# Projecting K ahead of Q, evacuating on VectorE, and projecting most of Q and all of V inside the first part of attention, in a causal transformer layer

## The chip, the cores and the metric

The kernel is one program that runs on the 8 cores of one Trainium2 chip. Each core computes two of the 16 sequences, one after the other, with no exchange between cores. The metric is device time in microseconds (us) of the slowest core, as a median of runs.

## The reference

One layer: causal attention with 16 heads, a layer norm over input plus attention, then a quantised linear layer and a second layer norm.

```python
def _L0_attn_ref(x, WQ, WK, WV, WO):            # x: (16, 2048, 1024), 16 heads of 64
    Q = _split_heads(x @ WQ.T, h)
    K = _split_heads(x @ WK.T, h)
    V = _split_heads(x @ WV.T, h)
    scores = jnp.einsum('bhqd,bhkd->bhqk', Q, K) / jnp.sqrt(jnp.float32(dk))
    scores = jnp.where(causal, scores, NEG)
    m = jnp.max(scores, axis=-1, keepdims=True)
    e = jnp.exp(scores - m)
    attn = e / jnp.sum(e, axis=-1, keepdims=True)
    out = jnp.einsum('bhqk,bhkd->bhqd', attn, V)
    return out @ WO.T
def _L0_ffn_ref(x, w_int8, weight_scale, bias):
    w_deq = w_int8.astype(jnp.float32) * weight_scale
    x_norm = simple_rms_norm(x)
    x_q = activation_quant(x_norm)
    return jnp.einsum('bsd,od->bso', x_q, w_deq) + bias
x = _layernorm(x + _L0_attn_ref(x, ...), axis=-1)
x = _layernorm(x + _L0_ffn_ref(x, ...), axis=-1)
```

## The kernel before

Every sequence ("batch" below) has S = 2048 rows and D = 1024 columns. The instruction stream of each engine is written out by hand: `emit(engine, fn)` appends work, `W(engine, key, val)` appends one wait of that engine on a semaphore (each call is an instruction of its own, also where the value has been reached long before), and `bump` counts what has been signalled. So an engine's order is the order of the calls. PE is TensorE, DVE VectorE, ACT ScalarE, POOL GpSimd.

A batch runs through three functions. `ph1` loads the transposed input `xT` (four DMAs) and the weights for Q and K into the two weight buffers `wslot[0]` (wslotA in the trace) and `wslot[1]` (wslotB), and projects. A projection group is 8 matmuls that accumulate a 128x512 tile in one PSUM bank. Q has 64/2 = 32 groups and K has 32; they rotate over PSUM banks 0 to 3, and ACT copies each tile to `QT` or `KT` (line 283). Then `ph1` defines `emit_vgroup`, a group of the V projection: 8 matmuls (line 318) into bank 6 or 7 and a DVE copy into `Vx` (line 331). There are 32 of these. WV is loaded to `wslot[0]` once Q's last matmul is done.

`ph2` is attention. It loops over four query chunks `qc` of 512 rows, over eight head pairs `hp`, and over `n_kt = 4*qc + 4` key tiles `k`: 4, 8, 12 or 16 steps in a head pair, 320 in a batch, 32 of them in qc = 0. Step `u` does this:

- PE: `emit_st` waits until ACT has read the same half of the double buffer two steps earlier (one wait), then issues two score matmuls (64 rows, up to 512 columns, line 381) into PSUM banks 2p and 2p+1, p = u % 2. In the last four steps of a head pair the columns shrink: 512, 384, 256, 128.
- ACT: exp of the scores into `PT` (line 482 at full width, line 493 narrower).
- POOL: in the last four steps of a head pair, the causal mask on two 128x128 blocks (line 507).
- PE: two steps later, `emit_pv` (line 399) multiplies with `Vx` into banks 4 and 5, after a wait on the mask of an earlier step.

At the end of a head pair PE waits for the last exps and masks, issues the remaining small products, and DVE normalises them into `o_ring` (lines 544 to 557). In qc = 0 three V groups follow each head pair (eight V groups stand ahead of the first); in qc >= 1 a transpose of an earlier chunk's output follows (`emit_trans`, line 425). The second linear layer's weights are loaded to `wslot[1]` as `ph2` begins, WO to `wslot[0]` after the first head pair of qc = 1; both DMAs are issued by POOL. `ph45` is the output projection, the norms and the quantised layer; the change does not touch it.

Of the kernel before, what the change touches and what calls it, by code (L numbers as in the profile page):

```python
# [38 lines left out]
def build_nc():  # L39
# [13 lines left out]
    with ExitStack() as ctx:  # L53
# [164 lines left out]
        def ph1(b, v_ready, prev_t_end, prev_v_end, prev_s_end):  # L218
# [10 lines left out]
            xt_done = ctr["gx"]  # L229
# [12 lines left out]

            wq_done = wload(wq_h, 0, prev_t_end)
            wk_done = wload(wk_h, 1, prev_t_end)

            s_evac = {}
            v_evac = {}
            half = 0
            q_last_mm = 0
# [3 lines left out]
            for proj, (wdone, slot, dest) in enumerate(  # L253
                    ((wq_done, 0, QT), (wk_done, 1, KT))):
                W("t", wdone[0], wdone[1])
                if proj == 0:
                    W("t", "gx", xt_done)
                    W("t", "v", v_ready)
                    W("t", "v", prev_v_end)
                    W("t", "s", prev_s_end)  # L260
                for dt in range(8):
                    for sch in range(4):
                        if half >= 4:
                            W("t", "s", s_evac.get(half - 4))
                        def f(eng, dt=dt, sch=sch, half=half, slot=slot):
                            out = pslot(half)
                            for kt in range(8):
                                lhsT = wslot[slot][
                                    :, kt * 1024 + dt * 128:
                                    kt * 1024 + dt * 128 + 128]  # L270
                                rhs = xT[:, kt * 2048 + sch * 512:
                                         kt * 2048 + (sch + 1) * 512]
                                mm = eng.matmul(out, lhsT, rhs,  # L273
                                                start=(kt == 0),
                                                stop=(kt == 7),
                                                skip_group_check=True)
                                if kt == 7:
                                    mm.then_inc(sem_t, 1)
                        emit("t", f)
                        mmv = bump("t")  # L280
                        W("s", "t", mmv)
                        def f3(eng, dt=dt, sch=sch, half=half, dest=dest):
                            eng.copy(dest[:, dt * 2048 + sch * 512:  # L283
                                          dt * 2048 + (sch + 1) * 512],
                                     pslot(half)).then_inc(sem_s, 1)
                        emit("s", f3)
                        s_evac[half] = bump("s")
                        half += 1
                if proj == 0:
                    q_last_mm = ctr["t"]  # L290

            wv_done = wload(wv_h, 0, q_last_mm)
# [10 lines left out]
            def emit_vgroup(g):  # L303
                st, dc = g // 2, g % 2
                n = ppu["n"]
                ppu["n"] += 1
                phh = n % 2
                if g < 2:
                    W("t", wv_done[0], wv_done[1])
                W("t", "v", ppu["ev"].get(n - 2))  # L310
                def f(eng, st=st, dc=dc, phh=phh):
                    out = pp[:, phh * 512:(phh + 1) * 512]
                    for kt in range(8):
                        lhsT = xT[:, kt * 2048 + st * 128:
                                  kt * 2048 + st * 128 + 128]
                        rhs = wslot[0][:, kt * 1024 + dc * 512:
                                       kt * 1024 + (dc + 1) * 512]
                        mm = eng.matmul(out, lhsT, rhs, start=(kt == 0),  # L318
                                        stop=(kt == 7),
                                        skip_group_check=True)  # L320
                        if kt == 7:
                            mm.then_inc(sem_t, 1)
                emit("t", f)
                mmv = bump("t")
                W("v", "t", mmv)
                def f2(eng, st=st, dc=dc, phh=phh):
                    dst = ap(Vx, st * 1056 + dc * 8 * 66,
                             (16896, 128), (66, 8), (1, 64))
                    src = ap(psall, 3072 + phh * 512, (4096, 128),
                             (64, 8), (1, 64))  # L330
                    eng.tensor_copy(dst, src).then_inc(sem_v, 1)  # L331
                emit("v", f2)
                val = bump("v")
                ppu["ev"][n] = val
                v_upto[st] = val

            qk_last_s = s_evac[63]
            return qk_last_s, vones, emit_vgroup, v_upto

        def ph2(b, wait_s0, vones, emit_vg, v_upto):  # L340
# [11 lines left out]
            w8_done = wload2(w8_h, 1, ctr["t"])  # L352
# [9 lines left out]
            for g in range(8):  # L362
                emit_vg(g)
            vg_next = 8
            prev_evac = max(vones, v_upto[3])

            def emit_st(qc, hp, k, p, wait_s):
                W("t", "s", wait_s)
# [73 lines left out]
            for qc in range(4):  # L442
                for hp in range(8):
                    if hp == 0:
                        W("t", "v", v_upto[min(4 * qc + 3, 15)])
# [6 lines left out]
                    for k in range(n_kt):  # L452
                        p = u % 2
                        pt = u % 4
                        wait_s = expv.get(u - 2)
                        if wait_s is None and u < 2:
                            wait_s = wait_s0
                        if u < 2:
                            W("t", "v", vones)
                        emit_st(qc, hp, k, p, wait_s)  # L460
                        stv = ctr["t"]
                        if k >= 2:
# [9 lines left out]
                            if mms:  # L472
                                W("t", "g", maskv.get(uu - 1))
                                if ku == 0:
                                    W("t", "v", prev_evac)
# [22 lines left out]
                        exp_last[p] = expv[u]  # L498
                        if k >= 4 * qc:
# [15 lines left out]
                    for ku in (n_kt - 2, n_kt - 1):  # L515
# [10 lines left out]
                        if mms:  # L526
                            emit_pv(qc, hp, mms, n_started, n_total)
# [39 lines left out]
                    if qc == 0:  # L567
                        while vg_next < min(32, 8 + 3 * (hp + 1)):
                            emit_vg(vg_next)
                            vg_next += 1  # L570
                    if qc >= 1:
# [3 lines left out]
                        if wo_done is None:  # L575
                            wo_done = wload2(wo_h, 0, ctr["t"])
# [360 lines left out]
        prev_s_end = 0  # L937
        for b in range(BPC):
            qk_s, vones, emit_vg, v_upto = ph1(b, v_ready, prev_t_end,
                                               prev_v_end, prev_s_end)  # L940
            (trans_done, wo_done, w8_done, exp_last,
             trans_ev) = ph2(b, qk_s, vones, emit_vg, v_upto)
# [4 lines left out]
            prev_s_end = ctr["s"]  # L947

# [65 lines left out]
```

## Time and profile before

| | us |
|---|---|
| median of two runs | 1715.0 (1714.69 to 1715.3) |
| the profiled execution | 1715.27 |
| its span on the slowest core, core 5 | 1713.4 |
| spans of the eight cores | 1697.5 to 1713.4 |
| mean granted TensorE clock by core | 0.799 to 0.817 of 2.4 GHz |

The profile is of core 5. In batch 0 the DMA of the first inputs lasts until 48 us, the Q and K projections until 161, eight V groups until 175, qc = 0 until 277, qc = 1 until 356, qc = 2 until 480, qc = 3 until 617 and `ph45` until 855; batch 1 repeats this. "The granted clock" is the share of full clock that TensorE was given: it is either 1.2 or 2.4 GHz, so 0.77 is a mix of both.

### The profile page before, as it was taken

How to read it: one execution, taken by the hardware profiler on the slowest of the kernel's cores; microseconds unless marked ns; L12 is line 12 of the kernel's file. 1: busy time of each engine (PE TensorE's matmuls, PEld its weight loads, DVE VectorE, ACT ScalarE, POOL GpSimd, SP SyncE). 2: the span in 40 equal slices, each digit the busy share in tenths (PEclk: the TensorE clock that was granted, in tenths of full speed). 3: DMA queues.
4: the chain of work that ended last, by engine and by line, in shares of the span. 5: the costliest groups of instructions: out<-in, count | busy, mean ns of one | idle time of the engine just before them, and what ended most of it. 6: DMA issues, size and time to landing. Idle time of an engine off the chain costs nothing.

```text
span 1713.4 us, 25217 instructions; the slowest of 8 cores (1697.5 to 1713.4 us)
## 1 busy us (share of the span) xinstructions
PE 1237.7 (72%) x8710; PEld 584.4 (34%) x8710; DVE 576.1 (34%) x1647; ACT 854.1 (50%) x1188; POOL 302.6 (18%) x599
## 2 busy tenths in 40 slices
PE   1899777877777776667409997877777777756664
PEld 0344333434344332222204443333443434322221
DVE  1000322211111148888600012322111111588886
ACT  0332224777788743444503322156777878334444
POOL 1000222222211211221200002232222121111112
PEclk9999876577778888888759997765677887888887
DMA  9331102000000002222192220020000000022211
GB/s 159 62 50 22 28 1 47 4 1 2 1 2 1 1 13 62 77 87 83 67 164 40 50 50 1 1 50 1 2 1 1 1 2 1 25 68 80 74 62 62
DMA packets 21917, 64.54 MB, mean 38 GB/s; under 512 B 1315, under 2 KB 1315, under 8 KB 21796
## 3 DMA queue, kind: packets, MB, share of 16 engines
q0 software_dynamic: 17184, 46.14, 12.9%
q1 hardware_dynamic: 4612, 16.78, 3.4%
q8 instruction: 76, 1.25, 0.3%
q14 instruction: 45, 0.37, 0.1%
HBM read 75.50 MB, written 16.78 MB: 54 GB/s over the span
## 4 chain that ended last, share of the span: by engine, by line
PE 40%; ACT 20%; DVE 14%; POOL 10%; issue 9%; DMA 5%; DVEq 1%; ACTq 0%; POOLq 0%
ACT PT L482 19%; PE psall L273 13%; POOL PT L507 9%; PE psall L318 8%; PE psall L641 8%; DMA wslotA<-wqt 5%; PE psall L381 5%; PE psall L399 4%; DVE dump L679 2%; DVE dumpb L682 2%; PE psall L425 2%; DVE st L685 1%; DVE st L686 1%; DVE z2x L842 1%; DVE z L842 1%
## 5 line engine op out<-in xcount | busy, mean ns | idle before, releaser
L482 ACT ACTIVATE PT<-psall,ebias 128x1024 bf16<-128x1024 f32 x448 | 468.5, 1116 | 308.8 <-PE psall L381 308.8
L381 PE MATMUL psall<-QT,KT 64*128 64x512 bf16 (+3 forms) x1280 | 280.9, 450 | 126.8 <-ACT PT L482 112.1
L399 PE MATMUL psall<-Vx,PT 128*128 128x65 bf16 x4352 | 303.0, 216 | 85.4 <-POOL PT L507 83.9
L507 POOL TENSOR_TENSOR PT<-PT,mask 128x128 bf16<-128x128 bf16 x512 | 200.6, 425 | 703.6 <-ACT PT L482 703.3
L399 PEld LDWEIGHTS psall<-Vx,PT 128*128 128x128 bf16 x4352 | 210.0, 110 | 246.9 <-issue 235.9
L544 DVE RECIPROCAL rinv<-psall 128x4 f32<-128x4 f32 x64 | 11.7, 183 | 636.5 <-PE psall L399 636.5
L641 PE MATMUL psall<-wslotA,OT 128*128 128x512 bf16 x512 | 159.1, 483 | 80.5 <-DVE z L842 44.5
L273 PE MATMUL psall<-xT,wslotA 128*128 128x512 bf16 x512 | 114.6, 388 | 86.3 <-DMA wslotA<-wqt 86.3
L331 DVE CAST Vx<-psall 128x512 bf16<-128x512 f32 x64 | 44.3, 692 | 382.6 <-PE psall L318 381.2
L825 PE MATMUL psall<-wslotB,qT 128*128 128x512 bf16 x512 | 123.8, 398 | 42.3 <-ACT qT L809 42.3
L318 PE MATMUL psall<-wslotA,xT 128*128 128x512 bf16 x512 | 147.0, 457 | 0.0
L381 PEld LDWEIGHTS psall<-QT,KT 64*128 64x128 bf16 x1280 | 68.2, 97 | 228.5 <-issue 206.6
L493 ACT ACTIVATE PT<-psall,ebias 128x768 bf16<-128x768 f32 (+2 forms) x192 | 120.8, 697 | 0.0
L641 PEld LDWEIGHTS psall<-wslotA,OT 128*128 128x128 bf16 x512 | 59.3, 119 | 179.4 <-issue 151.2
L273 PE MATMUL psall<-xT,wslotB 128*128 128x512 bf16 x512 | 110.8, 379 | 0.0
L557 DVE TENSOR_SCALAR o_ring<-psall,rinv 128x64 bf16<-128x64 f32 x512 | 104.3, 277 | 5.8 <-issue 0.8
L273 PEld LDWEIGHTS psall<-xT,wslotA 128*128 128x128 bf16 x512 | 50.8, 100 | 151.2 <-issue 93.5
L283 ACT CAST QT<-psall 128x512 bf16<-128x512 f32 x64 | 37.5, 586 | 117.7 <-PE psall L273 117.7
L825 PEld LDWEIGHTS psall<-wslotB,qT 128*128 128x128 bf16 x512 | 49.7, 101 | 106.5 <-issue 58.4
L726 ACT ACTIVATE sc<-sc 128x2 f32<-128x2 f32 x32 | 6.5, 204 | 158.9 <-DVE sc L717 158.9
L318 PEld LDWEIGHTS psall<-wslotA,xT 128*128 128x128 bf16 x512 | 56.8, 113 | 82.6 <-issue 44.7
L783 POOL TENSOR_TENSOR x1b<-x,bias_b 128x1024 f32<-128x1024 bf16 x32 | 68.4, 2137 | 73.5 <-DVE qint L773 68.1
(95 smaller groups left out, 886.1 us busy)
## 6 DMA issues: line engine op xcount, KB each, us to landing
xstg<-x SPq DMA_DIRECT2D x32, 512.0 KB, 3.7
y<-outst POOLq DMA_DIRECT2D x32, 512.0 KB, 3.0
xT<-xt POOLq DMA_DIRECT2D x8, 1024.0 KB, 21.4
wslotA<-wqt POOLq DMA_DIRECT2D x2, 2048.0 KB, 41.5
wslotB<-wkt POOLq DMA_DIRECT2D x2, 2048.0 KB, 52.2
wslotA<-wvt POOLq DMA_DIRECT2D x2, 2048.0 KB, 16.5
wslotB<-w8t POOLq DMA_DIRECT2D x2, 2048.0 KB, 16.1
wslotA<-wot POOLq DMA_DIRECT2D x2, 2048.0 KB, 15.0
```

What stands on the lines that cost most here:

```text
L273: mm = eng.matmul(out, lhsT, rhs, start=(kt == 0), stop=(kt == 7), skip_group_check=True)
L318: mm = eng.matmul(out, lhsT, rhs, start=(kt == 0), stop=(kt == 7), skip_group_check=True)
L331: eng.tensor_copy(dst, src).then_inc(sem_v, 1)
L381: last = eng.matmul(out, lhsT, rhs, start=True, stop=True, skip_group_check=True)
L399: last = eng.matmul(out, lhsT, rhs, start=(i_glob < 2), stop=(i_glob >= n_total - 2), skip_group_check=True)
L482: eng.activation(PT[:, pt * 1024:(pt + 1) * 1024], psall[:, p * 1024:(p + 1) * 1024], AF.Exp, bias=ebias[:, :], scale=0.125).then_inc(sem_ ...
L493: eng.activation(dst, src, AF.Exp, bias=ebias[:, :], scale=0.125).then_inc(sem_s, 1)
L507: last = eng.tensor_tensor(blk, blk, mask01[:, :], ALU.mult)
L557: last = eng.tensor_scalar(o_ring[:, ro + qt * 1024 + h * 64: ro + qt * 1024 + h * 64 + 64], ps[:, qt * 65:qt * 65 + 64], rinv[:, s_ * 4 + ...
L641: mm = eng.matmul(out, lhsT, rhs, start=(dt == 0), stop=(dt == 7), skip_group_check=True)
L783: eng.tensor_tensor(x1b2h(t), x1[:, t * 1024:(t + 1) * 1024], bias_b2[:, 0:1024], ALU.add).then_inc(sem_m, 1)
L825: mm = eng.matmul(out, lhsT, rhs, start=(dt == 0), stop=(dt == 7), skip_group_check=True)
```

## The change

- K is projected ahead of Q. Its weights are loaded first, and its groups run with the column chunk `sch` outside and `dt` inside. Q's first column chunk (8 groups) follows. The other 24 Q groups are emitted inside attention, two after each of the steps u = 0 to 11.
- `proj_group` evacuates with DVE in place of ACT. It waits on whatever last read its PSUM bank, which is kept in `slotc`. A Q group emitted in step u uses bank 2p or 2p+1, which hold the scores of step u, so it waits for the exp of step u.
- All 32 V groups are emitted inside attention, two after each of the steps u = 0 to 15. None stands ahead of attention, and none follows a head pair.
- `emit_st` waits four times where it waited once: on `slotc` of its two banks (in most steps the same value of the same semaphore), on the evacuation of its K chunk and on that of its Q chunk. In qc = 0 the products wait for their V tile as well.
- WV goes to `wslot[1]` after K's last matmul, WO to `wslot[0]` after Q's last group in qc = 0, and the second layer's weights to `wslot[1]` after the first head pair of qc = 1. POOL still issues all three.
- The memset of the ones column of `Vx` stands behind 40 evacuations on DVE; it gates the first two score steps.

```diff
+            evK = {}
+            evQ = {}
+            H = {"half": 0, "first_ev": True, "q_all": None}
+            slotc = [None, None, None, None]
...
+            def proj_group(slot, dt, sch, dest, ev):
+                j = H["half"] % 4
+                if slotc[j] is not None:
+                    W("t", slotc[j][0], slotc[j][1])
+                def f(eng, dt=dt, sch=sch, j=j, slot=slot):
+                    out = pslot(j)
+                    for kt in range(8):
...
+                emit("t", f)
+                mmv = bump("t")
+                W("v", "t", mmv)
+                if H["first_ev"]:
+                    H["first_ev"] = False
+                    W("v", "t", prev_t_end)
+                    W("v", "g", prev_m_end)
+                def f3(eng, dt=dt, sch=sch, j=j, dest=dest):
+                    eng.tensor_copy(dest[:, dt * 2048 + sch * 512:
+                                         dt * 2048 + (sch + 1) * 512],
+                                    pslot(j)).then_inc(sem_v, 1)
+                emit("v", f3)
+                ev[(dt, sch)] = bump("v")
+                slotc[j] = ("v", ev[(dt, sch)])
+                H["half"] += 1
+
+            W("t", wk_done[0], wk_done[1])
+            W("t", "gx", xt_done)
+            W("t", "v", v_ready)
+            W("t", "v", prev_v_end)
+            W("t", "s", prev_s_end)
+            for sch in range(4):
                 for dt in range(8):
...
+                    proj_group(1, dt, sch, KT, evK)
+            k_last_mm = ctr["t"]
+            wv_done = wload(wv_h, 1, k_last_mm)
+
+            W("t", wq_done[0], wq_done[1])
+            for dt in range(8):
+                proj_group(0, dt, 0, QT, evQ)
+            qrem = [(dt, sch) for sch in (1, 2, 3) for dt in range(8)]
+            qst = {"i": 0}
+
+            def emit_qgroup():
+                dt, sch = qrem[qst["i"]]
+                qst["i"] += 1
+                proj_group(0, dt, sch, QT, evQ)
+                if qst["i"] == len(qrem):
+                    H["q_all"] = ctr["t"]
...
-                        rhs = wslot[0][:, kt * 1024 + dc * 512:
+                        rhs = wslot[1][:, kt * 1024 + dc * 512:
...
-            w8_done = wload2(w8_h, 1, ctr["t"])
+            w8_done = None
...
-            for g in range(8):
-                emit_vg(g)
-            vg_next = 8
-            prev_evac = max(vones, v_upto[3])
-
-            def emit_st(qc, hp, k, p, wait_s):
-                W("t", "s", wait_s)
+            vg_next = 0
+            prev_evac = vones
+
+            def emit_st(qc, hp, k, p):
+                for j in (2 * p, 2 * p + 1):
+                    if slotc[j] is not None:
+                        W("t", slotc[j][0], slotc[j][1])
+                W("t", "v", evK[(hp, k // 4)])
+                W("t", "v", evQ[(hp, qc)])
...
-                        wait_s = expv.get(u - 2)
-                        if wait_s is None and u < 2:
-                            wait_s = wait_s0
                         if u < 2:
                             W("t", "v", vones)
-                        emit_st(qc, hp, k, p, wait_s)
+                        emit_st(qc, hp, k, p)
...
+                                if qc == 0:
+                                    W("t", "v", v_upto.get(ku))
...
+                        slotc[2 * p] = ("s", expv[u])
+                        slotc[2 * p + 1] = ("s", expv[u])
+                        if qc == 0:
+                            nst = u + 1
+                            while qst["i"] < min(nq, 2 * nst):
+                                emit_qgroup()
+                            if qst["i"] == nq and wo_done is None:
+                                wo_done = wload2(wo_h, 0, P["H"]["q_all"])
+                            while vg_next < min(32, 2 * nst):
+                                emit_vg(vg_next)
+                                vg_next += 1
...
-                    if qc == 0:
-                        while vg_next < min(32, 8 + 3 * (hp + 1)):
-                            emit_vg(vg_next)
-                            vg_next += 1
                     if qc >= 1:
...
-                        if wo_done is None:
-                            wo_done = wload2(wo_h, 0, ctr["t"])
+                        if w8_done is None:
+                            w8_done = wload2(w8_h, 1, ctr["t"])
```

## Rows read from the trace of the kernel before

**Rows 1.** Busy time by stage of batch 0; first line: the columns.
```profile
core 5: us, PE busy (x) PEld busy (x) DVE busy (x) ACT busy (x) POOL busy (x), PEclk, DMA share, GB/s
48.00:175.00 127.00, 126.51 (x576) 56.75 (x576) 4.92 (x8) 38.79 (x65) 1.75 (x2) 1.00 0.28 43
175.00:277.00 102.00, 78.92 (x420) 33.08 (x420) 31.63 (x105) 22.83 (x32) 25.06 (x64) 0.77 0.04 7
277.00:356.00 79.00, 60.55 (x568) 31.16 (x564) 17.95 (x78) 56.71 (x64) 25.18 (x63) 0.59 0.16 28
356.00:480.00 124.00, 94.40 (x978) 49.55 (x978) 22.27 (x99) 97.80 (x104) 25.91 (x67) 0.72 0.01 1
480.00:617.00 137.00, 101.84 (x1146) 54.49 (x1142) 17.76 (x80) 113.31 (x121) 25.11 (x64) 0.81 0.01 1
```

**Rows 2.** Chain that ended last: start us, us, what. Projections and V bursts, batch 0.
```profile
48.31 112.69 PE psall L273 x512
161.01 13.83 PE psall L318 x64
...
181.27 7.41 PE psall L318 x24
...
268.90 7.93 PE psall L318 x24
```

**Rows 3.** The same chain: start of attention, then the second head pair of qc = 0.
```profile
174.93 0.70 DVE Vx L331
175.63 0.35 issue
175.97 0.41 PE psall L381 x2
...
189.11 1.12 ACT PT L482
...
193.64 0.27 PE psall L399 x2
```

**Rows 4.** PE in order of time, the same head pair: its first scores.
```profile
188.62 0.55 PE L381 MATMUL psall<-QT,KT 64*128 64x512 bf16 x4
```

**Rows 5.** Instructions of qc = 0 by shape: count, busy us, mean ns, idle before.
```profile
L331 DVE CAST Vx<-psall 128x512 bf16<-128x512 f32 x25 | 17.3, 692 | 32.9 <-PE psall L318 32.9
...
L482 ACT ACTIVATE PT<-psall,ebias 128x1024 bf16<-128x1024 f32 x8 | 8.9, 1114 | 82.4 <-PE psall L381 82.4
L493 ACT ACTIVATE PT<-psall,ebias 128x768 bf16<-128x768 f32 x8 | 7.1, 893 | 0.0
...
L493 ACT ACTIVATE PT<-psall,ebias 128x512 bf16<-128x512 f32 x8 | 5.5, 688 | 0.0
L493 ACT ACTIVATE PT<-psall,ebias 128x256 bf16<-128x256 f32 x8 | 3.8, 474 | 0.0
```

**Rows 6.** Other engines in order of time: ACT's table load; DVE's memset of `Vx`.
```profile
51.97 1.28 ACT L283 ACT_TABLE_LOAD   x1 [51.97 <-PE psall L273]
...
14.80 0.27 DVE L296 MEMSET Vx<- 128x256 bf16 x1 [0.86 <-issue]
```

**Rows 7.** DMA issues at 100 to 182 us: KB, us to landing.
```profile
wslotA<-wvt POOLq DMA_DIRECT2D x1, 2048.0 KB, 18.1
```

**Rows 8.** Chain inside a head pair of qc = 3: one wait of PE on an exp.
```profile
535.05 1.11 ACT PT L482
536.16 0.14 issue
```

**Rows 9.** PE in order of time, qc = 3: two steps, clock low; two steps, high.
```profile
529.03 0.60 PE L381 MATMUL psall<-QT,KT 64*128 64x512 bf16 x2
...
530.12 0.60 PE L381 MATMUL psall<-QT,KT 64*128 64x512 bf16 x2
...
535.29 0.39 PE L381 MATMUL psall<-QT,KT 64*128 64x512 bf16 x2 [0.27 <-ACT PT L482]
...
536.30 0.39 PE L381 MATMUL psall<-QT,KT 64*128 64x512 bf16 x2 [0.26 <-ACT PT L482]
```

## Prediction: time of the changed kernel, and why

> **What bounds the kernel now.** I read the stages by time first, then the chain that ended last, then PE in order of time. The reader is to see in the first that no engine is busy throughout attention (PE in 102 of 137 us of qc = 3, ACT in 113 [rows 1]), so that each stage must be read by what its chain waits for. Three kinds of stage are touched.
>
> The projections are PE and nothing else. PE is busy for 126.5 of 127 us at full clock, and 512 matmuls take 112.69 us; the 64 matmuls of eight V groups take 13.83 us, 0.216 us each [rows 1, 2]. ACT's copies are hidden under this.
>
> The stage qc = 0 alternates. After each burst of 24 V matmuls comes a stretch in which PE waits for exp and mask. It lasts from 188.68, where the burst of 7.41 us ends, to 193.91, where the next starts: 5.23 us [rows 2, 3]. Eight such stretches cost 42 us. They also cost clock: the stage has 0.77 of it, and the eight bursts take 7.4, 7.9, 6.5, 7.4, 7.9, 6.5, 7.4 and 7.9 us, 58.9 in all (first and last in [rows 2]), where 192 x 0.216 = 41.5 would do. So 17.4 us a batch is the low clock after the idle stretches.
>
> In qc = 1 to 3, ACT and PE hand each other the two score buffers. At full clock a step takes 1.00 us and PE idles 0.26 of it for the exp, so ACT bounds it; at the low clock a step takes 1.09 us and PE has no gap [rows 9].
>
> **The change, part by part.** All sums are for one batch and then doubled. They start from the profiled execution, 1715.27 us, which stands 0.3 us above the median.
>
> *Projections.* K and Q's first chunk are 40 groups, 320 matmuls. Taking 192 x 0.216 = 41.5 from the 112.69 leaves 71.2 us. A DVE evacuation takes 0.69 us and a group 8 x 0.216 = 1.73, so DVE keeps up and four banks hide it [rows 2, 5]. The start waits for the same inputs and one weight matrix as before. WV lands 18.1 us after its issue [rows 7]; between K's last matmul and the first V group stand 13.8 us of Q, the first scores and exp, and two Q groups, 20 us, so it is just covered. If it slipped, each us would show once. The later weight loads have stages to spare, and POOL issues one of them where it issued one before.
>
> *Start of attention.* Before, last matmul to first score took 1.1 us: the copy of 0.70, then 0.35 for three waits [rows 3]. Now the memset of 0.27 [rows 6] and more waits follow the copy: 1.6 us. ACT's table load of 1.28 us, hidden under the projections in batch 0 [rows 6], now stands ahead of the first exp: once 1.3 us.
>
> *qc = 0, head pairs 0 to 2.* Each of the 12 steps has scores, exp, then 32 matmuls. The Q group waits for the exp, since it takes the bank. From first score to exp is 0.49 us in full width [rows 3, 4], and I take 0.41 on average for narrower ones; the exps are 1.11 + 0.89 + 0.69 + 0.47 [rows 5]; back to PE is 0.14 [rows 8]. Four steps: 4 x 0.41 + 3.16 + 4 x 0.14 = 5.4 us. The bursts hide the masks. With 0.2 for the last products a head pair costs 5.6 + 128 x 0.216 = 33.2, three cost 99.6.
>
> *Head pair 3.* V only, banks of its own, so the exp is hidden: 64 x 0.216 + 1.2 for scores and products = 15.0.
>
> *Head pairs 4 to 7.* Nothing fills them. They cost the old 5.23 plus three more waits of PE ahead of their first score and a low clock's slower score: 5.7 each, 22.8.
>
> Sum from 48.3 us to qc = 1: 71.2 + 1.6 + 99.6 + 15.0 + 22.8 = 210.2. Before it was 228.5 (48.3 to 276.8, the end of the last burst [rows 2]). **Gain 18.3 a batch, 36.6 less 1.3 for the table, so 35.3.** Nearly all of it is clock, on the reading that PE's short stretches of 0.9 to 1.7 us between bursts are not what the 5.2 us ones are, and that the Q and V bursts run at 0.216. If instead the clock fell as it does now, the gain would be gone (a rival).
>
> *The four waits of `emit_st`.* One satisfied wait costs PE's queue something: three in a row stand for 0.35 us in the chain, one for 0.14, so each further one costs 0.105 [rows 3, 8]. Three more are 0.32 us ahead of each score pair. Where PE's queue is ahead of its array (during transposes and bursts) they cost nothing; behind an exp that has just ended they are on the way. The buffer loop spans two steps: exp 1.11 + 0.14 + scores 0.39 + about 0.10 to the exp = 1.74 against 2.00 at full clock, so 0.32 more makes 2.06, or 1.03 a step, +0.03. At the low clock it is 1.11 + 0.14 + 0.60 + 0.10 = 1.95 against 2.18, so 2.27, 1.14 a step, +0.05 [rows 8, 9]. At each head pair's start there is no such slack: about 0.1 to 0.16 for the first score, and 0.3 to 0.4 for the third, which waits on the first exp. At its end POOL's eight masks run back to back and shift no further. With 4, 8 and 12 steps between, a head pair loses 0.75, 0.9 and 0.95 us in qc = 1, 2, 3. **Eight of each: 20.8 a batch, 41.6.** Bounds: nothing, if the queue hides all the waits; 288 steps x 0.16 = 46 a batch, 92, if the loop had no slack anywhere.
>
> By the Trainium skill (Advanced Engine Details and Errata, section Network/Comms) a sequencer's read of a semaphore takes 50 to 100 ns. Three such reads would be 0.15 to 0.3 us, and as an estimate from that page the time would be 1710 to 1729; the 0.105 of the trace lies just above the page's figure.
>
> *Clock in qc = 2 and 3.* It is 0.59, 0.72 and 0.81 in the three stages [rows 1]. Longer steps hold more idle time of PE, and qc = 1, which has the shortest head pairs and so the largest part of waiting, has the lowest clock; so part of the high stretches may go. A high step that turns low costs 1.14 - 1.03 = 0.11. All of them, about half of 224 a batch, would be 25 to 27 us in both batches; I take 10. Bounds: 0 and 27.
>
> **Sum:** 1715.3 - 35.3 + 41.6 + 10 = 1731.6, and I say 1731, 0.9% slower than the median. The output projection and the norms stay.
>
> **Rivals.**
> 1. *The extra waits are free* (faster). They would have to be passed while PE's array works. For it: PE runs ahead in bursts. Against: in [rows 9] PE idles on the exp at full clock, and the queue can't pass a wait behind the one that blocks it. Time: 1715 - 35 = 1680, with some loss left 1680 to 1695. It decides at a cost per wait under about 0.03 us: then the loss is below 12 us. Chance 0.14.
> 2. *The clock falls in the new bursts* (slower). For it: after 5.2 us stretches it falls eight times a batch, and each burst loses 17.4/8 = 2.2 us. Against: the new stretches are a third as long. If all 24 bursts lost 2.2, the time is 1731 + 52 = 1783; with a third of them, 1749. The point is where a 1.7 us stretch already brings 1.2 GHz. Chance 0.08. The Trainium skill has a rule on this side (TensorE: Matmul & The Clock Gate, section A second HAM failure mode: psum-queue depth-cycling): a matmul kernel that cycles PSUM banks, with short idles between groups, can swing between the two clocks. That is the shape of the new bursts; the projections in [rows 1] cycle four banks at 1.00 of the clock, but without idles.
> 3. *The clock stays low through qc = 2 and 3*: the 27 in place of 10, with a somewhat larger wait loss, 1748 to 1755. For it: qc = 1 sits near 0.5 already. Chance 0.15.
> 4. My forecast, 1708 to 1748: 0.63.
>
> **How the numbers follow.** About 2% (34 us) is what a measurement of this kernel tells from no change; the edges are 1681 and 1749. Faster: half of rival 1 lies below 1681 or near it, and I give 0.06. Slower: rival 2's upper part, half of rival 3, and a tail of the forecast, together 0.18. Within 2%: 0.76. The range of 1696 to 1757 leaves out most of rivals 1 and 2, 0.2 in all; the forecast's own range is 1708 to 1748.
>
> **What the changed profile would show.** (a) The chain from 48 us to qc = 1 is 210 us in place of 228, and Q and V bursts run at 0.216 a matmul with a clock near 1.0 until head pair 4. (b) From exp to score the "issue" piece is 0.46 in place of 0.14. (c) Steps in qc = 3 last 1.03 and 1.14. (d) The clock in qc = 2 and 3 is below 0.72 and 0.81. (e) One table load of 1.3 us ahead of batch 0's first exp. If (b) shows less than 0.2, or if a burst of 32 matmuls takes over 8 us, the forecast is wrong.

## The result, and the profile after

| | before | after |
|---|---|---|
| median, us | 1715.3 | 1739.5 |
| ratio, 95% interval | | 1.0142 (1.0128 to 1.0156) |
| profiled execution, span of the slowest core | 1713.4 (core 5) | 1737.4 (core 6) |

The changed kernel is 1.4% slower. The forecast was 1731, 0.9% slower. The stages, in us, as means over the eight cores for batch 0 / batch 1 (from the first matmul of the projections to the first exp, then from first exp to first exp of each chunk; the last chunk to its last exp; "rest" up to the next batch or the end):

| | projections | qc = 0 | qc = 1 | qc = 2 | qc = 3 | rest |
|---|---|---|---|---|---|---|
| before | 128.2 / 129.5 | 96.6 / 96.0 | 81.1 / 80.7 | 113.1 / 113.2 | 142.7 / 143.1 | 286.0 / 248.5 |
| after | 75.4 / 75.6 | 144.1 / 144.1 | 85.5 / 85.3 | 120.6 / 120.3 | 151.6 / 151.5 | 285.6 / 246.1 |

Projections and qc = 0 together became 5.3 and 5.8 us shorter, the other three chunks 20.8 and 20.1 us longer. For the slowest cores alone it is 8.5 and 9.2 us shorter against 21.1 and 20.8 us longer.

The stages of the changed kernel, batch 0, core 6 (columns as in [rows 1]):

```profile
48.00:120.00 72.00, 71.28 (x320) 31.66 (x318) 27.60 (x40) 0.00 (x0) 0.88 (x1) 1.00 0.31 47
120.00:268.00 148.00, 122.98 (x676) 55.46 (x676) 52.60 (x133) 26.26 (x33) 26.64 (x65) 0.91 0.11 18
268.00:353.00 85.00, 63.92 (x576) 33.75 (x574) 18.98 (x87) 59.20 (x64) 26.27 (x65) 0.56 0.16 26
353.00:474.00 121.00, 94.74 (x898) 49.70 (x896) 19.73 (x89) 93.90 (x96) 25.34 (x64) 0.63 0.01 1
474.00:626.00 152.00, 115.88 (x1203) 61.71 (x1202) 19.44 (x86) 127.12 (x128) 23.69 (x60) 0.72 0.01 2
```

On these two cores the clock of qc = 0 rose from 0.77 to 0.91, and that of qc = 2 and 3 fell from 0.72 and 0.81 to 0.63 and 0.72. As means over the eight cores, between the exps that bound the stages, it is 0.82, 0.56, 0.74 and 0.79 in qc = 0 to 3 before, and 0.91, 0.54, 0.65 and 0.72 after.

PE in order of time inside a head pair of qc = 3, changed kernel (it answers to the last two of [rows 9]):

```profile
541.28 0.39 PE L412 MATMUL psall<-QT,KT 64*128 64x512 bf16 x2 [0.19 <-issue]
...
542.38 0.39 PE L412 MATMUL psall<-QT,KT 64*128 64x512 bf16 x2 [0.36 <-issue]
...
543.39 0.39 PE L412 MATMUL psall<-QT,KT 64*128 64x512 bf16 x2 [0.26 <-issue]
...
544.45 0.39 PE L412 MATMUL psall<-QT,KT 64*128 64x512 bf16 x2 [0.32 <-issue]
```

The steps are 1.10, 1.01 and 1.06 us. What is to be seen is the bracket: before, PE's idle time ended with ACT's exp; now it ends with "issue". The exp that the step waits for has ended 0.46 us before its first score (median in qc = 3, all cores), where the kernel before has 0.144 at full clock. In that time PE works through waits that are already satisfied.

The chain that ended last, changed kernel: start of attention, two of the first bursts, then the third score pair of qc = 1.

```profile
47.57 71.73 PE psall L266 x320
...
119.39 0.69 DVE QT L280
120.08 0.86 issue
...
121.79 0.41 PE psall L412 x2
122.27 1.28 ACT L512
123.56 1.12 ACT PT L512
124.82 5.04 PE psall L266 x16
129.85 3.45 PE psall L336 x16
...
134.72 3.61 PE psall L266 x16
138.34 3.45 PE psall L336 x16
...
158.07 0.70 DVE Vx L349
...
269.18 0.49 issue
269.67 0.61 PE psall L412 x2
```

What held back the first score is DVE's memset behind the copy, with idle time of its own in the bracket:

```profile
120.95 0.27 DVE L314 MEMSET Vx<- 128x256 bf16 x1 [0.86 <-issue]
121.79 0.39 PE L412 MATMUL psall<-QT,KT 64*128 64x512 bf16 x2 [2.50 <-DVE Vx L314]
```

The last two lines of the chain are the wait cost in one place: 0.49 us from exp to score where one wait stands for 0.14 [rows 8].

### The profile page after: what moved, and what is told of

Same layout as the page of the kernel before. It is cut to its first block, busy times and chain, and to the rows that moved or that the text cites. A ratio compares the mean times of both kernels' runs of the same rounds, so it can differ in the third digit from the quotient of the medians.

```text
span 1737.4 us, 27201 instructions; the slowest of 8 cores (1729.0 to 1737.4 us)
## 1 busy us (share of the span) xinstructions
PE 1257.0 (72%) x8710; PEld 601.2 (35%) x8710; DVE 663.8 (38%) x1775; ACT 808.6 (47%) x1060; POOL 305.5 (18%) x599
## 4 chain that ended last, share of the span: by engine, by line
PE 39%; DVE 19%; ACT 18%; POOL 9%; issue 7%; DMA 5%; DVEq 1%; ACTq 0%; POOLq 0%
ACT PT L512 16%; PE psall L266 14%; POOL PT L548 9%; PE psall L680 8%; PE psall L336 6%; PE psall L412 6%; DMA wslotB<-wkt 5%; PE psall L430 4%; DVE o_ring L600 4%; DVE dump L718 2%; DVE dumpb L721 2%; DVE OT L467 2%; DVE st L724 1%; DVE st L725 1%; DVE z L881 1%
## 5 line engine op out<-in xcount | busy, mean ns | idle before, releaser
L512 ACT ACTIVATE PT<-psall,ebias 128x1024 bf16<-128x1024 f32 x448 | 485.1, 1113 | 225.7 <-PE psall L412 218.1
L412 PE MATMUL psall<-QT,KT 64*128 64x512 bf16 (+3 forms) x1280 | 304.4, 478 | 135.4 <-DVE OT L467 48.5
L430 PE MATMUL psall<-Vx,PT 128*128 128x65 bf16 x4352 | 314.5, 223 | 59.1 <-POOL PT L548 55.1
L430 PEld LDWEIGHTS psall<-Vx,PT 128*128 128x128 bf16 x4352 | 222.6, 114 | 232.6 <-issue 218.6
L680 PE MATMUL psall<-wslotA,OT 128*128 128x512 bf16 x512 | 160.2, 486 | 79.3 <-DVE z L881 44.0
L523 ACT ACTIVATE PT<-psall,ebias 128x768 bf16<-128x768 f32 (+2 forms) x192 | 131.3, 686 | 168.8 <-PE psall L412 164.5
L266 PE MATMUL psall<-xT,wslotB 128*128 128x512 bf16 x512 | 115.2, 389 | 85.5 <-DMA wslotB<-wkt 85.5
L412 PEld LDWEIGHTS psall<-QT,KT 64*128 64x128 bf16 x1280 | 78.3, 98 | 246.2 <-issue 230.0
L266 PE MATMUL psall<-xT,wslotA 128*128 128x512 bf16 x512 | 120.6, 392 | 24.0 <-ACT PT L523 13.3
L680 PEld LDWEIGHTS psall<-wslotA,OT 128*128 128x128 bf16 x512 | 59.6, 120 | 179.1 <-issue 151.6
L336 PE MATMUL psall<-wslotB,xT 128*128 128x512 bf16 x512 | 115.8, 379 | 0.0
L266 PEld LDWEIGHTS psall<-xT,wslotB 128*128 128x128 bf16 x512 | 51.0, 100 | 150.7 <-issue 93.3
L280 DVE CAST KT<-psall 128x512 bf16<-128x512 f32 x64 | 44.3, 692 | 153.0 <-PE psall L266 153.0
L280 DVE CAST QT<-psall 128x512 bf16<-128x512 f32 x64 | 44.3, 692 | 106.9 <-PE psall L266 106.9
## 6 DMA issues: line engine op xcount, KB each, us to landing
xT<-xt POOLq DMA_DIRECT2D x8, 1024.0 KB, 21.1
```

What stands on the lines that cost most here:

```text
L266: mm = eng.matmul(out, lhsT, rhs, start=(kt == 0), stop=(kt == 7), skip_group_check=True)
L280: eng.tensor_copy(dest[:, dt * 2048 + sch * 512: dt * 2048 + (sch + 1) * 512], pslot(j)).then_inc(sem_v, 1)
L336: mm = eng.matmul(out, lhsT, rhs, start=(kt == 0), stop=(kt == 7), skip_group_check=True)
L412: last = eng.matmul(out, lhsT, rhs, start=True, stop=True, skip_group_check=True)
L430: last = eng.matmul(out, lhsT, rhs, start=(i_glob < 2), stop=(i_glob >= n_total - 2), skip_group_check=True)
L512: eng.activation(PT[:, pt * 1024:(pt + 1) * 1024], psall[:, p * 1024:(p + 1) * 1024], AF.Exp, bias=ebias[:, :], scale=0.125).then_inc(sem_ ...
```

## The experiments

**One wait a step again.** Which part of the change lengthens qc = 1 to 3?

```diff
-                        W("t", slotc[j][0], slotc[j][1])
-                W("t", "v", evK[(hp, k // 4)])
-                W("t", "v", evQ[(hp, qc)])
+                        W("t", slotc[j][0], slotc[j][1], once=True)
+                W("t", "v", evK[(hp, k // 4)], once=True)
+                W("t", "v", evQ[(hp, qc)], once=True)
```

`once=True` leaves a wait out if that engine has already waited for as high a value of the semaphore.

> The changed kernel, in which emit_st leaves out each wait whose value PE has already waited for on that semaphore; nothing else differs. My theory (three satisfied waits a step, 0.105 us each, lengthen the buffer loop of qc = 1 to 3): each score pair of qc 1 to 3 is again behind one wait, the stages fall back to 81, 113 and 143 us, about 20.5 us a batch, and the time is about 1699, 0.99 of the kernel before. Rival (the longer stages come from the clock, which fell in qc = 2 and 3 for another reason, or from the weight load that moved into qc = 1): the waits hardly matter and the time stays at 1735 to 1740.

Measured: 1693.9 us, ratio to before 0.9875 (0.9835 to 0.9914). The stages qc = 1, 2, 3 are 81.1, 113.1, 142.7 and 81.2, 113.4, 142.9 us, the old ones to 0.5 us. So leaving the waits out takes back 40.4 of the 40.9 us that the two batches had lost there. The clock of qc = 2 and 3 is back as well (0.74 and 0.79, means over the cores), so it fell by no cause of its own, and the moved weight load costs nothing that shows. The kernel as a whole is 45.6 us faster than the changed one, 5 more than I had forecast: qc = 0 takes 141.7 and 141.9 us where it took 144.1, so the waits cost some 4.6 us there too.

**The same waits in the kernel before.**

```diff
                 W("t", "s", wait_s)
+                if qc >= 1:
+                    for _ in range(3):
+                        W("t", "s", wait_s)
```

> The kernel before, with the one wait of emit_st written four times in qc = 1 to 3 and nothing else. My theory: its stages qc = 1, 2, 3 become those of the changed kernel, 85, 120.5 and 151.5 us, and the time 1715 + 41 = 1756. Rival (waits are nearly free and something else in the change made the stages longer): under 1725.

Measured: ratio 1.0217 (1.0163 to 1.0271, from two runs), profiled execution 1752.4 us. Stages 84.9, 120.6, 151.1 and 85.6, 120.3, 151.0, within 0.6 us of the changed kernel's. Its clock in qc = 2 falls too: 0.60 to 0.68 on the eight cores in both batches, where the kernel before has 0.74 on every core. Nothing but the waits differs, so the fall of the clock follows from them.

**Six more, and one more.** The same edit with `range(6)`, and with one line.

> The kernel before, with the one wait of emit_st written seven times in qc = 1 to 3. My theory (a loop of two steps with slack): with three more waits part of the cost lay in the slack (0.26 us at full clock), with six more it lies outside, so the cost per wait rises: full-clock steps go to 1.19 us and low-clock ones to 1.30, stages qc = 1, 2, 3 to about 95, 135 and 172 us, 65 a batch, and the time to about 1845. Rival (each wait costs the same everywhere): twice the cost of three, 1797.

> The kernel before, with the one wait of emit_st written twice in qc = 1 to 3. With three more waits the steps of qc = 3 took 1.052 and 1.140 us, so the buffer loop of two steps has 2.104 - 0.318 = 1.79 us of its own at full clock and 1.96 at the low one, against 2.00 and 2.19 measured without them. My theory (slack of 0.2 us): one more wait leaves the steps at 0.997 and 1.093 and costs only at the start of each head pair, 0.1 to 0.2 us: 5 to 9 us in all, about 1722. Rival (each wait costs the same wherever it stands): a third of the 41 us, 1729.

Measured: six give 1862.3 us (a single run, without an interval), stages 95.6, 138.5, 176.8; one gives ratio 1.003 (1.0019 to 1.0042), stages 81.8, 114.0, 144.0. The table has, over all cores, the time from the end of a head pair's first exp to its third score (median, qc = 1 to 3), where PE has nothing left to do but wait; the mean step from one exp's start to the next in seven steps in the middle of qc = 3's head pairs, at either clock; and the added time of the three stages, as the mean of the batches:

| extra waits | exp to third score, us | step at 2.4 GHz, us | step at 1.2 GHz, us | added in qc = 1 to 3, us a batch |
|---|---|---|---|---|
| 0 | 0.144 | 1.000 | 1.093 | |
| 1 | 0.250 | 1.006 | 1.094 | 2.8 |
| 3 (changed kernel) | 0.462 | 1.047 | 1.159 | 20.4 |
| 6 | 0.795 | none left | 1.301 | 73.8 |

(The last column is the sum of the stages less 336.95, the mean of before.) The steps are means because with extra waits long and short ones alternate (1.50 and 1.13 us with six), so that a median depends on the steps chosen; the 1.052 and 1.140 in the expectation are such medians. The wait itself has a fixed price, 0.106 us for each of the first three (0.250 - 0.144, and (0.462 - 0.144)/3). What it costs the stage is another matter: one wait costs 2.8, three cost 6.8 each, six cost 12.3 each. It is a loop with slack. At 1.2 GHz the slack is to be seen directly: in the middle of qc = 3 the score pair starts 0.361 us after its exp without extra waits, 0.364 with one, and 0.462 with three, so the first is hidden behind PE's own work and the others are not. With six, no step in the middle ran at full clock any more: the mean clock is 0.70 to 0.71 against 0.80 to 0.82. That is more than I had forecast, 1845, since I had counted some full-clock steps.

**V ahead of Q within a step.**

```diff
                             nst = u + 1
-                            while qst["i"] < min(nq, 2 * nst):
-                                emit_qgroup()
-                            if qst["i"] == nq and wo_done is None:
-                                wo_done = wload2(wo_h, 0, P["H"]["q_all"])
                             while vg_next < min(32, 2 * nst):
                                 emit_vg(vg_next)
                                 vg_next += 1
+                            while qst["i"] < min(nq, 2 * nst):
+                                emit_qgroup()
+                            if qst["i"] == nq and wo_done is None:
+                                wo_done = wload2(wo_h, 0, P["H"]["q_all"])
```

> The changed kernel with one thing swapped: in steps 0 to 15 of qc = 0 the two V groups are emitted ahead of the two Q groups. V's banks are free, so its 3.45 us run while ACT does the exp that the Q groups wait for. My theory (each of the 12 steps with Q groups has PE idle for the exp, 1.75, 1.42, 1.15 and 0.89 us in a head pair, 5.2 in all): 3 x 5.2 = 15.6 us a batch less, qc = 0 from 144 to 128 us, time about 1708. Rival (these idle stretches are not what keeps qc = 0 long, but the clock or the evacuations on DVE): under 5 us a batch, 1730 or more.

Measured: 1716.8 us, ratio to before 1.0007 (0.999 to 1.0023); qc = 0 takes 132.4 and 130.8 us, 11.7 and 13.3 less. So PE's idle time over the exp accounts for most of the 15.6 us a batch that I had forecast. The chain of this kernel, core 0, names two things that I had not counted:

```profile
105.83 17.14 DMA wslotB<-wvt
123.10 5.30 PE psall L336 x16
...
209.73 3.47 PE psall L266 x16
213.24 0.47 issue
213.73 0.94 POOL wslotA L378
214.68 0.83 POOL PT L548 x2
216.24 0.61 PE psall L412 x2
216.85 4.95 PE psall L336 x16
```

V now starts early enough to wait for WV's DMA. And POOL's issue of WO's load (0.94 us) waits for Q's last group and holds back the mask of that step. PE idles near 3 us there, and the next burst starts at the low clock (4.95 where 3.45 is normal). In the changed kernel the V burst stands behind Q's last group and covers this.

**V spread over qc = 0.** The first experiment and the last one together, with `min(32, 2 * nst if nst <= 4 else nst + 4)` for V.

> The changed kernel with the redundant waits of emit_st left out, V groups ahead of Q groups, and V spread: two groups in each of the first four steps, then one in each of steps 4 to 27. So head pairs 4 to 6 have a V group over each exp too. My theory: 41 us less for the waits, and qc = 0 loses nearly all idle time, from 144 to about 113 us a batch, together about 1638. Rival (the projections inside attention are bound by something other than PE's idle time over exps and masks, such as the clock or DVE's copies): the two parts don't add up, and it is 1665 or more.

Measured: ratio 0.9633 (0.9582 to 0.9685), profiled span 1649.6 us. qc = 0 takes 120.9 and 118.9 us, not 113. The direction held, and the size was over-estimated as in the step before. POOL's issue of WO's load stands in the same step as there; what part of the missing 6 to 8 us a batch it is, no run shows.

**V spread, in the kernel before, alone.**

```diff
                         exp_last[p] = expv[u]
+                        if qc == 0 and vg_next < 32:
+                            emit_vg(vg_next)
+                            vg_next += 1
...
-                    if qc == 0:
-                        while vg_next < min(32, 8 + 3 * (hp + 1)):
-                            emit_vg(vg_next)
-                            vg_next += 1
```

> The kernel before with one thing moved: the 24 V groups that follow the head pairs of qc = 0 in threes stand one after each of its first 24 steps. Q, K, ACT's copies and the single wait of emit_st stay. My theory (idle time of PE over exps and masks, and the low clock after it, is what makes qc = 0 long, and V groups over the exps are enough to remove it): 41.4 us of matmuls, some 12 of scores and products, two bare head pairs of 5.5, so 65 where 96 us were, time about 1655. Rival (the changed kernel's gain needs Q inside attention, or ACT freed of its copies): under 10 us a batch, 1695 or more.

Measured: 1647.2 us, ratio 0.9596 (0.9577 to 0.9616). qc = 0 falls from 96.6 and 96.0 to 64.5 and 63.2 us. Time beyond 0.216 us a matmul in its V bursts is 0.1 to 0.8 us a batch; in the kernel before it is 7.0 to 17.3, depending on the core. The clock of the stage is 0.96 on the slowest core:

```profile
175.00:240.00 65.00, 59.68 (x417) 26.52 (x415) 29.40 (x96) 24.93 (x32) 24.80 (x62) 0.96 0.07 13
```

So neither Q inside attention nor DVE's copies are needed for the gain.

**No wait of PE twice, in the kernel before.** The rule of the first experiment, for all of PE's waits.

> The kernel before, in which every wait of PE for a value that it has already waited for on the same semaphore is left out (the mask wait in the steps that have no mask, above all). My theory (a satisfied wait costs only where PE's queue has no slack): these stand behind the scores, where PE's queue has time to spare, so the gain is 0 to 8 us, 1707 to 1715. Rival (each satisfied wait costs 0.105 us wherever it stands, some 200 of them a batch): 20 us a batch, about 1675.

Measured: 1707.4 us, ratio 0.9947 (0.993 to 0.9964), at the upper end of the gain that I gave and far from the rival's 1675. Nearly all of it is in qc = 1 to 3, 3.9 us a batch. The place decides what a wait costs.

**ACT's copies back.** K and Q's first chunk are copied by ACT, the other 24 Q groups by DVE.

```diff
-                    proj_group(1, dt, sch, KT, evK)
+                    proj_group(1, dt, sch, KT, evK, "s")
...
-                proj_group(0, dt, 0, QT, evQ)
+                proj_group(0, dt, 0, QT, evQ, "s")
```

> The changed kernel, with K and Q's first column chunk copied out of PSUM by ACT as before, the 24 Q groups inside attention still by DVE. My theory (of the move to DVE only the start of attention is on the path): batch 0 no longer has ACT's table load of 1.28 us ahead of its first exp, and the memset no longer stands behind the last copy; 1.5 to 2 us less in batch 0 and up to 0.5 in batch 1, about 1737.5. Rival (the move to DVE holds PE up within the projections): the projections get shorter by more than 2 us a batch, 1734 or less.

Measured: 1728.9 us, ratio to before 1.0077 (1.0064 to 1.0089), some 10 us faster than the changed kernel (9.3 in the mean span of the cores). I was wrong by far. The rival's time came true and its cause did not: from the first to the last projection matmul it is 71.3 and 71.0 us here, 71.1 and 71.3 in the changed kernel. What went is the pause behind them. From the start of the last projection matmul to the first score it is 0.31 us where the changed kernel has 2.9; the table load went in batch 0; and qc = 0 itself is 2.4 and 1.1 us shorter. The chain of this kernel, core 3:

```profile
120.30 0.29 ACT QT L277
120.58 0.20 issue
120.78 1.13 ACT PT L523
121.91 0.14 issue
122.04 3.61 PE psall L266 x16
```

The Q half of the first burst takes 3.61 us, on all eight cores in batch 0, and not the 5.04 to 6.57 of the changed kernel. In batch 1, where the table load stays and the pause is 3.25 us, it takes 5.30 on seven cores. So the pause at the start of attention had cost clock as well.

**Q in the idle ends of head pairs.** PE waits for nothing twice. Q's groups use banks 6 and 7 as V's do. The second chunk stands in steps 28 to 31 and at four ends of qc = 0, the third and fourth at the ends of qc = 1 and 2. WO's load moves with the last Q group, to the head pairs of qc = 2. The second version is its base, with Q and WO's load as in the changed kernel. Of the edits of the first, the one at the ends:

```diff
...
+                    if (qc == 0 and hp < 4) or qc in (1, 2):
+                        emit_qgroup()
                     for ku in (n_kt - 2, n_kt - 1):
```

> Built on the version with V spread over qc = 0 and V ahead: PE waits for no value twice, and Q's groups use PSUM banks 6 and 7 like V's, so none waits for an exp. Q's second column chunk stands in qc = 0 (four in steps 28 to 31, four at the ends of head pairs), its third and fourth at the ends of the head pairs of qc = 1 and 2, ahead of the products that wait for POOL's masks. My theory: 16 groups a batch go into idle time of about 2 us at each end, 16 x 1.73 = 28 us less a batch of which the low clock gives some back, and qc = 0 loses its waits for the exp: 1590 to 1605. Rival (the ends of head pairs are bound by PE at the low clock, so the groups add their own time there): about the 1650 of the spread version.

> The version with V spread over qc = 0, where in addition PE waits for no value twice on any semaphore; it differs from the version with Q at the ends of head pairs (1570.6) only in where the Q groups stand and which PSUM banks they use. My theory (most of the step from 1651 to 1570.6 comes from Q's place and banks): the left-out waits bring what they brought in the kernel before, some 9 us, so about 1642. Rival (the waits left out everywhere are what made that version fast): under 1615.

Measured: 1570.6 us, ratio 0.9151 (0.9135 to 0.9168), and 1642.9 for the base, ratio 0.9568 (0.9554 to 0.9583). So Q's place and banks, with WO's load behind them, brought 72 us, more than I had forecast; the runs don't part the three. qc = 0 takes 86.3 and 84.0 us where the base has 120.7 and 119.6. qc = 1 and 2 carry eight more groups each and take 81.9, 109.1 and 80.2, 109.5, against 79.3, 111.2 and 79.5, 112.0 of the base. The stages of qc = 1 and 2, batch 0, core 5, first of the base:

```profile
245.00:324.00 79.00, 59.72 (x575) 30.75 (x572) 19.20 (x87) 56.63 (x65) 25.95 (x66) 0.63 0.16 28
324.00:435.00 111.00, 84.38 (x897) 44.67 (x896) 19.80 (x88) 89.49 (x97) 24.69 (x65) 0.74 0.01 1
```

And with Q's groups in them:

```profile
210.00:292.00 82.00, 64.60 (x647) 33.70 (x646) 24.76 (x96) 55.99 (x65) 26.13 (x66) 0.87 0.16 27
292.00:401.00 109.00, 87.77 (x955) 47.38 (x954) 24.58 (x96) 87.58 (x95) 23.67 (x61) 0.88 0.01 1
```

The clock is 0.87 and 0.88, where it is 0.63 and 0.74 in the base. So 16 groups, 28 us of matmuls a batch at 0.216 each, cost next to nothing in these stages: PE's idle time over the masks became work, and the clock rose. The runs don't part these two. In qc = 3, which holds no Q groups, the clock is 0.80 against 0.78, and its time is the same to 0.5 us.

## Why the prediction was right, and where it was not

*The sign and the time.* 1731 against 1739.5. The mechanisms were right in the main, but the time came out close in part by luck: the gain up to qc = 1 was put 17.6 us too large, and waits and clock together 9.7 us too large (51.6 against 41.9 on the slowest cores), so that the two errors partly cancelled: 1731.6 + 17.6 - 9.7 is 1739.5.

*The four waits of `emit_st`: 41.6 us, and 10 for the clock.* The first experiment gives 40.4 for both together. The mechanism was right: a further wait is 0.106 us, the loop has slack, and the knee is where it was put. The steps lengthened a little more than forecast, to 1.047 and 1.159 us where 1.03 and 1.14 stood. A head pair lost 0.56, 0.91 and 1.08 us in qc = 1, 2 and 3, with the clock's part in it, where the forecast had 0.75, 0.9 and 0.95 without it. So the shortest head pairs, which are nearly all start and end, were over-estimated. An estimate of the clock's part: leave out the first two and the last two steps of each head pair of qc = 1 to 3. Of the others that ran wholly at one clock, 52% were at full clock before and 40% after. There are 192 of them a batch and a low one is 0.11 us longer, so 0.12 x 192 x 0.11 = 2.5 us a batch, and about 5 of the 41 are clock, not 10. The two parts can't be told apart more closely, as no run has the three waits without the fall of the clock.

The figure of the Trainium skill (Advanced Engine Details and Errata, section Network/Comms: 50 to 100 ns to read a semaphore) lies a little under the 0.106 that the traces show for each further wait.

*The gain up to qc = 1: 35.3 us.* This is the term that was mis-sized most: 17.7 us on the slowest cores, 11.1 in the mean. By its own steps, for batch 0 of core 6 (forecast, then measured): projections 71.2, 71.7; start 1.6, 2.5; head pairs 0 to 2 with the table load 100.9, 106.7; head pair 3 15.0, 15.8; head pairs 4 to 7 22.8, 23.0. The sum is 211.5 against 219.8.

- The start: 0.86 us of "issue" stood between DVE's copy and the memset. It is in the bracket of the very row that I quoted for the memset [rows 6], and I read only its duration. With the rest of the pause it cost clock too: the Q half of the first burst took 5.04 us and not 3.61. The run with ACT's copies shows that this part of the change cost some 10 us in all, where I had 2.3: 1.3 for the table load and 0.5 a batch for memset and waits.
- Head pairs 0 to 2: the low clock in the first burst of head pair 0, and in that of head pair 1 (5.30), 3.1 us; the last products of head pair 0 wait for a V tile that has only just been projected, 0.70 for the copy and about 1.3 in all, which I did not count. The 16 matmuls with which a burst begins take 3.61 us and not 16 x 0.216 = 3.46, near 1.9 in the 12 bursts. Together these are 6.3 us where the head pairs came out 5.8 over the forecast, so the rest of them was a little shorter.
- The waits: the first experiment takes 2.4 and 2.2 us a batch off qc = 0 by leaving them out. I had counted them at the start and in head pairs 4 to 7 alone.
- The low clock before: I took 17.4 us from core 5. It was 17.3 and 16.3 there, but it lies anywhere between 7.0 and 17.3 over the cores and batches, for the same work. In the changed kernel it is 2.5 to 4.9, Q's bursts included. The mean gain is therefore smaller than that of the slowest core.

*The rivals.* The waits were not free. The clock did not fall in the new bursts as a rule: it was 0.95, 0.95 and 1.00 in head pairs 0 to 2. Over all cores and batches, a burst with Q began at full clock in 160 of 160 cases in which PE had been without projection matmuls for 0.88 to 1.93 us, at the low clock in 5 of 16 after 3.3 us (head pair 1), and in 16 of 16 after 5.5 us (the start of attention). So the second rival's point, a stretch of 1.7 us that already brings 1.2 GHz, was not reached. The psum-queue rule of the Trainium skill (TensorE: Matmul & The Clock Gate, section A second HAM failure mode: psum-queue depth-cycling) did not show here between such bursts of 7.07 us. The third rival's price did not come: the clock did fall in qc = 2 and 3 (0.63 and 0.72), as the forecast itself had it, but that cost about 5 us by the estimate above and not 27.

*The signs named ahead.* (a) missed, 220 us and not 210, and two bursts were low; (b) right, 0.49 in the chain and 0.462 as the median; (c) right to 0.02; (d) and (e) right, the table load with 1.28 us. The last sentence named a burst of 32 matmuls over 8 us as a sign of a wrong forecast, and that sign did show: the first burst of attention took 8.47 to 10.02 us on every core in both batches, and the first of head pair 1 took 8.75 in 5 cases of 16. It came from the pauses of 5.5 and 3.3 us and not from the 0.9 to 1.9 us between the other bursts, so it cost about 3 us a batch and not the 2.2 us of each of 24 bursts for which it was meant.

*What I had not asked.* The gain that this change was near to, V over the exps, needs one moved line: the kernel before with V spread alone is 4% faster.

## What to carry to other kernels

Count the waits in front of the instruction that a loop across two engines turns on, and leave out those that an earlier wait of the same engine implies; compare the sum with the slack of the loop, since the first wait may be free and the next is not. Put independent matmuls where PE waits for exp or mask, one group at a time and with buffers of their own, rather than in bursts between such stretches: here they filled the idle time, and the clock of the stages that held them rose (0.82 to 0.94 in qc = 0 with V spread, 0.63 and 0.74 to 0.87 and 0.88 in qc = 1 and 2 with Q), while qc = 3, which held none, stayed at 0.78 to 0.80. When a row is read for its duration, read the idle time in its bracket too.

## What was not expected of the hardware

- The same qc = 0 of the kernel before takes 92.9 to 100.8 us on the eight cores of one execution (batch 0), and time at the low clock in its V bursts accounts for it: 9.5 to 17.3 us. With V spread, the cores agree to 0.8 us in that.
- Waits that are satisfied lower TensorE's granted clock: 0.74 in qc = 2 with one wait, 0.60 to 0.68 with four, in an otherwise unchanged kernel. None of the first five steps of a head pair of qc = 2 and 3 ran wholly at full clock in either kernel. The ninth step of a head pair of qc = 3 did so always before, and in 64% of the cases after.
- The same 0.106 us a wait is nearly free as one more and costs 73.8 us a batch as six more.
- A memset of 0.27 us on DVE is preceded by 0.86 us of "issue" in both kernels; what fills that time no run here shows.
